# Re-ordering the five engines around the gene sums: projection a pair ahead, sums ahead of the turn of heads, and new orders behind the sums

## The reference

```
h = einsum('bg,egp->bep', x, weight * mask) + bias      # x 64x5000, weight 16x5000x128: 41 MB
h = h + attention(layernorm(h))   # 16 positions per batch row, 8 heads of 16 (+2 rotary), causal
h = h + ffn(layernorm(h))         # 64 experts, top 2 by gate, 128->64->128 silu, plus a shared expert
```

## Time and profile before

| | us |
|---|---|
| median of 3 runs (252.67 to 255.78) | 253.7 |
| the profiled execution's own time | 254.11 |
| its span (first to last instruction) | 252.4 |
| busy in the span: PE, DVE, POOL, ACT | 184.7, 152.0, 144.1, 82.4 |
| mean granted TensorE clock | 0.891 |

### The profile page before, as it was taken

The page is one execution under the profiler, slowest core; times in us unless marked ns, Lnnn a source line. Parts: engine busy times, 40 slices in busy tenths (PEclk is TensorE's granted clock), DMA queues, the critical chain, the costliest instruction groups (busy, mean ns, idle before and its releaser), DMA issues.

```text
span 252.4 us, 6075 instructions
## 1 busy us (share of the span) xinstructions
PE 184.7 (73%) x2479; PEld 153.9 (61%) x2479; DVE 152.0 (60%) x366; ACT 82.4 (33%) x245; POOL 144.1 (57%) x117
## 2 busy tenths in 40 slices
PE   0057877279989789695896699388976987999810
PEld 0057866169878678584785488257755766678410
DVE  0024382975696888979939928768796249011291
ACT  2004200023343333341331232538664444335500
POOL 3326479259979779999678783103114242074570
PEclk9999999977999999999599599657996599999965
DMA  7999999999999999999999999593011128213432
GB/s 237 256 342 418 361 421 334 403 417 417 417 419 422 417 419 416 426 417 413 396 226 220 227 194 145 153 265 145 4 42 52 55 70 243 87 42 96 139 96 53
DMA packets 32981, 65.11 MB, mean 258 GB/s; under 512 B 2874, under 2 KB 25367, under 8 KB 32375
## 3 DMA queue, kind: packets, MB, share of 16 engines
q1 hardware_dynamic: 31416, 59.47, 71.5%
q10 hardware_dynamic: 576, 3.26, 3.1%
q0 software_dynamic: 960, 1.97, 3.0%
HBM read 56.96 MB, written 7.73 MB: 256 GB/s over the span
## 4 chain that ended last, share of the span: by engine, by line
PE 39%; DVE 19%; DMA 16%; SPq 8%; ACT 7%; issue 4%; POOL 3%; POOLq 1%; DVEq 0%; ACTq 0%
DMA ring<-in_L_tok_weight_dram 15%; PE bank L833 13%; PE bank L1021 4%; SPq L360 4%; PE bank L991 4%; DVE bank L1233 3%; DVE prod L1227 3%; DVE ring L1206 3%; DVE prod L1251 2%; DVE bank L1259 2%; PE bank L1005 2%; SPq L366 2%; PE bank L971 2%; PE bank L876 2%; POOL ring L529 2%
## 5 line engine op out<-in xcount | busy, mean ns | idle before, releaser
L464 POOL TENSOR_TENSOR ring<-ring,mask 128x896 f32<-128x896 f32 (+1 forms) x48 | 91.6, 1933 | 19.0 <-DMA ring<-in_L_tok_weight_dram 19.0
L833 PE MATMUL bank<-ring,xT 128*64 128x128 f32 x1248 | 83.8, 294 | 9.9 <-DVE ring L1206 7.6
L833 PEld LDWEIGHTS bank<-ring,xT 128*64 128x64 f32 x1248 | 76.4, 149 | 14.6 <-DVE ring L1206 9.2
L1206 DVE TENSOR_TENSOR ring<-ring,bank 128x1024 f32<-128x1024 f32 (+1 forms) x45 | 45.7, 1049 | 35.5 <-DMA ring<-in_L_tok_weight_dram 35.5
L453 POOL TENSOR_TENSOR rstd<-mv,half 128x1 f32<-128x1 f32 (+1 forms) x24 | 14.2, 599 | 38.9 <-DVE mv L1214 23.4
L529 POOL DMA_INDIRECT ring<-expert_outputs,slot_index x16 | 16.0, 1002 | 16.9 <-DMA expert_outputs<-ring 8.0
L484 POOL DMA_INDIRECT expert_inputs<-xf,slot_index x14 | 14.3, 1021 | 9.9 <-DVE slot_index L1311 6.9
L814 PE MATMUL bank<-cst,w 64*128 64x64 f32 x39 | 5.3, 328 | 16.1 <-DMA w<-in_x_dram 15.4
L1021 PE MATMUL bank<-w2p,ring 64*64 64x128 f32 (+1 forms) x256 | 14.5, 291 | 3.4 <-ACT ring L705 2.1
L506 POOL TENSOR_TENSOR mask<-ring,mask 128x256 f32<-128x256 f32 x8 | 6.0, 756 | 16.3 <-ACT ring L699 16.3
L991 PE MATMUL bank<-w,ring 128*64 128x128 f32 (+1 forms) x256 | 14.9, 298 | 0.3 <-POOL mask L506 0.3
(11 more groups left out here) (151 smaller groups left out, 302.6 us busy)
## 6 DMA issues: line engine op xcount, KB each, us to landing
ring<-in_L_tok_weight_dram SPq DMA_DIRECT2D x48, 832.0 KB, 13.2
expert_inputs<-w ACTq DMA_DIRECT2D x3, 1024.0 KB, 9.9
ring<-expert_inputs SPq DMA_DIRECT2D x6, 512.0 KB, 5.4
expert_outputs<-ring SPq DMA_DIRECT2D x12, 256.0 KB, 2.3
mask<-in_L_tok_mask_dram SPq DMA_DIRECT2D x3, 832.0 KB, 16.1
w<-in_x_dram SPq DMA_DIRECT2D x1, 1250.0 KB, 13.6
w2p<-in_L_ffn_w_dram SPq DMA_DIRECT2D x1, 1024.0 KB, 18.9
xT<-masks_dram SPq DMA_DIRECT2D x1, 1024.0 KB, 7.9
```

What stands on the lines that cost most here:

```text
L464: pool.tensor_tensor(unit(j, q, SPLIT(q // 2), UC), unit(j, q, SPLIT(q // 2), UC), mask[:, (m + SPLIT(q // 2)) * D:(m + UC) * D], ALU.mult ...
L833: last = pe.matmul(bank[0][64 * par:64 * par + 64, 0:D], xT[:, (UC * t + c) * B:(UC * t + c + 1) * B], unit(j, 2 * t + par, c, c + 1), sta ...
L1206: dve.tensor_tensor(both(j, t, a, b), both(j, t, a, b), m.rearrange("p (u f) -> p u f", u=1).to_broadcast([P, 2, (b - a) * D]), ALU.mult). ...
```

## The change

Four things change, and no arithmetic does.

1. In the loop PE transposes and projects pair c-1 at the end of every turn (behind step 10, and behind step 11), where it did pair c-2 at the start. `turn_qk(b)` then stands at the start, `qkv(b)` behind the first step of sums and `values(b)` behind the second. ACT, DVE and POOL follow in their own orders. DVE's `scores` is split into `multiply_keys` and `sum_scores`, with `choose(d)` and `place(d)` between them.
2. From c = 5 on (`HEADED`) PE does step 0 of the sums ahead of `turn_o(d)`; for smaller c it stands behind `attend(d)`.
3. The orders behind the sums are new on PE, ACT, DVE and POOL. The experts' work stands further forward on PE.
4. The gathers of all five pairs of the first round are issued ahead of the wait for the last group (`GATHERED_EARLY` 4 to 5).

```
-GATHERED_EARLY = 4
+GATHERED_EARLY = NCH1          # 5
+HEADED = 5
-POOL_SHARE = (3, 3)
-VECTOR_SHARE = (2, 1, 2, 1)
+POOL_SHARE = (1, 1, 4)
+VECTOR_SHARE = (2, 2, 1, 1)
 ...                            # POOL, loop
                 mask_pieces(POOL_SHARE[0])
-                if d >= 0:
-                    root_h2(d)
                 if b >= 0:
                     root_qk(b)
                 mask_pieces(POOL_SHARE[1])
+                if d >= 0:
+                    root_h2(d)
+                mask_pieces(POOL_SHARE[2])
                 if c >= 1:
                     root_h(c - 1)
 ...                            # PE, loop
+                project_a, qkv_b, attend_d = c >= 1, b >= 0, d >= 0
+                if c >= HEADED:
+                    sum_genes(c, 0)
                 if attend_d:
                     turn_o(d)
-                if project_b:
-                    turn_xn(b)
+                if qkv_b:
+                    turn_qk(b)
                 if attend_d:
                     attend(d)
-                if project_b:
-                    project(b)
-                for n in range(4):
-                    sum_genes(c, n)
+                if c < HEADED:
+                    sum_genes(c, 0)
+                if qkv_b:
+                    qkv(b)
+                sum_genes(c, 1)
                 if attend_d:
                     turn_xf(d)
-                if project_b:
-                    turn_qk(b)
-                sum_genes(c, 4)
+                if qkv_b:
+                    values(b)
+                sum_genes(c, 2)
                 if attend_d:
                     gate(d)
-                if project_b:
-                    qkv(b)
+                sum_genes(c, 3)
                 if attend_d:
                     rank_tokens(d)
-                sum_genes(c, 5)
-                if project_b:
-                    values(b)
-                for n in range(6, 12):
+                for n in range(4, 12):
                     sum_genes(c, n)
-                    if c == NCH - 1 and n == 10:
+                    if project_a and n == 10:
                         turn_xn(c - 1)
-                if c == NCH - 1:
+                if c == 1:
+                    pe.wait_ge(s_centred, 2)
+                if project_a:
                     project(c - 1)
 ...                            # DVE, loop
-                mask_pieces(VECTOR_SHARE[2])
+                if a >= 0:
+                    stats_h(a)
+                if b >= 0:
+                    multiply_keys(b)
                 if d >= 0:
                     choose(d)
-                if a >= 0:
-                    stats_h(a)
+                mask_pieces(VECTOR_SHARE[2])
                 if d >= 0:
                     place(d)
                 if b >= 0:
-                    scores(b)
+                    sum_scores(b)
                     less_max(b)
```

More of the change, by code:

```diff
@@ L1236, in scores @@
                 then(dve.memset(raw(j)[0:64].rearrange("p (h s) -> p h s", h=NH)[:, :, n - 1:n], NEG))
+            def scores(j):
+                multiply_keys(j)
+                sum_scores(j)
             def less_max(j):
@@ L1391, in _ @@
             j, k, l = NCH - 3, NCH - 2, NCH - 1
+            weigh_values(j)
             stats_h(l)
-            heads(j)
-            scores(k)
+            sum_heads(j)
+            weights(0, NCH1)
+            multiply_keys(k)
+            sum_scores(k)
             less_max(k)
             add_attended(j)
-            heads(k)
-            scores(l)
+            weigh_values(k)
+            sum_heads(k)
+            multiply_keys(l)
+            sum_scores(l)
             less_max(l)
@@ L1401, in _ @@
             add_attended(k)
-            heads(l)
+            weigh_values(l)
+            sum_heads(l)
             place(j)
@@ L1420, in _ @@
             dve.tensor_scalar(flag_i[:], flag[:, 0:1], float(SLOTS), None, ALU.is_gt).then_inc(s_flag, 1)
-            for g in range(GROUPS1, GROUPS):
-                mid(g)
+            mid(8)
+            mid(9)
+            mid(10)
+            mid(11)
             shared_mid(0)
```

246 lines of the change are left out of this document (127 added, 119 removed).

## The result

The changed kernel is slower: 261.6 us (260.87 to 264.35, four runs) against 253.2 for the kernel before (four runs), a ratio of 1.038, interval 1.027 to 1.050. On a second chip it was 260.4 us and 1.027 (1.019 to 1.034). The forecast was 249 with a range to 257, so it missed on the other side. The profiled execution took 261.2 (span 259.5) where before took 254.11 (252.4): 7.1 more, where 4.5 less was forecast, a miss of 11.6 us.

What follows compares the result with a forecast made beforehand. Bound first by the granted clock, half speed in six stretches, then by TensorE. Loop +2.8, behind the sums 1.7 - 9.0 = -7.3, the end 0: -4.5 from 254.11 profiled gives 249.6, as median 249.2, said 249; range 242.3 to 257.

Steps and rivals of the forecast that it cites:

- E: End of the projection of pair k, closing the loop: 157.95 us before, forecast at 160.75.
- the rival: In the loop: TensorE falls to half clock behind waits at turn starts; three such turns cost 7.9 us, 257; chance 0.14.
- a case that was given 0.09: Whole kernel slower than before, above 258.8: the rival plus some of little gain from the orders behind the sums; chance 0.09.
- The loop's chain: Turns c = 3 to 7, put together from measured stretches: 16.2, 16.5, 16.8, 17.2 and 19.05 us, sum 85.75.
- The third turn (c = 2): In the loop: 4.3 us lost, as 2.9 idle, 0.7 transposing and projecting pair 1, 0.7 products at half clock.
- GpSimd's lateness in c = 7: In the loop: one mask ahead of root_qk(5) makes it start 1.55 us later, so c = 7 takes 19.05.
- its 2.8 us: End of the loop later than before: 4.3 - 1.45 = 2.8 us.
- The rows at no cost: Behind the loop: first round's rows requested at about 162, turn_xs(0) reached at 167.3; cost 0, at most 1 us.
- probs(k): On ScalarE behind the sums: standing behind silu(0) and silu(1), with more table loads, it costs 3.1 us.
- The stretch without the late rows: From E to turn_o(l): 35.4 us where it took 33.7, 1.7 later.
- From turn_o(l) to round two: Up to round two's first transposition: 15.4 us where it took 24.4, 9.0 less.
- Round two and the end: From round two's first transposition to the span's end: the 36.3 us stay, and part 4 gains nothing.

Runs made afterwards that it cites:

- e16: The changed kernel without part 2, step 0 behind attend(d) in every turn (HEADED = 8): 260.3 to 263.6 us, ratio to before 1.033.
- e4: The changed kernel with step 0 of the sums ahead of turn_o from c = 2 on: 260.0 us, ratio to before 1.015.
- e18: The changed kernel with two of the loads of w2 issued behind the loads of the first round's rows: 258.1 us, ratio to before 1.020.
- e9: The changed kernel with idle products sized to TensorE's waits at the start of turns 2 to 7: 257.1 us, ratio to before 1.013.
- e14: e9 with w2 also loaded in long rows, so the output is not the reference's: 256.7 us, ratio to before 1.012.
- e15: e10 with idle products in the old loop, ahead of turn_o in turns 5 to 7 and ahead of turn_qk(k): 248.5 us, ratio to before 0.981.
- e6: The changed kernel with TensorE's two short waits at the start of a turn filled with sums from c = 2 on: 259.9 us, ratio to before 1.028.
- e1: The kernel before with the new orders behind the sums and part 4, its old loop kept: 250.8 us, ratio to before 0.982.
- e10: e1 with mid(6) ahead of scatter(k) on GpSimd, nothing else: 249.3 us, ratio to before 0.981.
- e2: The changed kernel's new loop with the old orders behind the sums (parts 1 and 2 alone): ratio to before 1.011.
- e17: e15 with two loads of w2 issued behind the loads of the first round's rows, as in e18: 243.5 us, ratio to before 0.957.

## Why the prediction was wrong, step by step

**Where the miss of 11.6 us lies.** 6.4 us are in the loop (5.8 in turns 3 to 7, 0.6 ahead of them), 3.1 from E to turn_o(l), 1.4 from there to round two, 0.7 behind. The two steps that failed are the full clock assumed for `turn_qk`, `attend` and the steps of sums in each turn, and the cost of nothing put on the first round's rows.

**The half clock was the rival, and it was the case.** I gave it 0.14 because 2.33 us had left the clock full and 2.40 had not, and took my waits of 2.0 to 2.2 to be on the safe side. As a threshold on one wait this fails: it fell behind 2.05, and behind 0.84 and 0.66 together, and stayed behind 2.09 (e16), 1.33 with 0.66 (e4) and even 3.43 (e18). The rival's place and its decision rule were wrong, its size nearly right: 5.8 us over turns 3 to 7 (91.55 against 85.75), where it had 7.9. It stood at 257 in the forecast; 261.6 needed the late rows besides, a case that was given 0.09. The Trainium skill's rule, "TensorE: Matmul & The Clock Gate", section "HAM oscillation — how this bites in real kernels", that a loop which waits in each pass starts each pass cold, describes turns 2 to 4 here, though the example there has longer waits, for DMAs. The trace agrees in turns 2 to 4 (1.97 us for 1.09, behind 2.88, 2.61 and 2.05); in turns 5 to 7 the fall comes 1 to 2.4 us behind the second wait, in the middle of the chain.

**The loop's chain** was right once the clock was full: e9's five turns sum to 86.5, forecast 85.75. The third turn (c = 2), priced at 4.3, ended at 75.6, where 70.7 + 4.3 = 75.0 was meant, and c = 1 had already ended 0.9 later. This agreement holds only with the half clock in that turn, which the price had in part: in e14's execution without it the turn took 3.0 us less. GpSimd's lateness in c = 7 stood as said: `root_qk` starts right behind a mask, 19.0 us in e9 for 19.05. So at nearly full clock the new loop ends at 162.3 (e9), and the old one, with its waits filled too, at 155.0 (e15): the order of part 1 is the longer one by itself, as the forecast had said of it with its 2.8 us.

**The rows at no cost.** This step failed. I let the request for the last units come 7 us later and the transfers end at 163 to 165. But the weights are queued behind the request that the end of turn c = 5 releases, and that turn ended 12.9 us later (129.82 for 116.94): the late turns win time, the early ones have lost theirs by then. Of this the forecast had 7, by its own turns; the rest is for the most part the half clock again, which made turns 3 to 5 longer by 5.1 us. The transfers ended some 12 us later, and the request for the rows followed about 2 us behind (158 to 159.4 before, 170 to 171.9 after, 166 to 168.3 in e9; the ends are read from the DMA share in steps of 2 us). The step didn't hold even by its own numbers: with transfers that end at 163 to 165, a request 2 us behind them and the 4.3 us from request to `turn_xs(0)` (171.88 to 176.15), the rows are there at 169 to 171, and `turn_xs(0)` was to be reached at 167.3. That is a wait of 2 to 4 us, and 2.81 came; the forecast had shifted the request with E and not with the transfers. e18 shows the price: 38.5 to 35.3 us for the stretch.

**probs(k)** behind the silus cost 3.1 us in the forecast and 2.86 in the trace. The stretch without the late rows took 35.3 us in e18, 36.2 in e6 and 36.4 in e1, against 35.4: right to 1 us, and the 0.1 of e18 is luck.

**From turn_o(l) to round two** 15.4 was forecast, 16.8 came. `mid(6)` was put at 8.6 us behind turn_o(l) and ended at 8.4; the rest is the clock again (0.90 in the stretch), which falls behind the wait of 3.44: `up(7)` takes 1.46 us for 1.09. In e1 it falls there too, 1.3 us later. In e18, with the same orders and a wait of 3.43, it stayed at 1.00 and the stretch took 15.25. In e10, which took the wait away, it was 13.5.

**Round two and the end**, part 4 among them, changed by 0.7. The last gather starts 28.9 us behind the first transposition of round two, and 28.6 before: the gathers issued earlier gain nothing, as said. Part 4 was not run by itself.

**What stays open.** Why the clock falls behind waits of 0.8 and 0.7 in one turn and not behind 2.1 or 3.4 elsewhere; and the rest of what e1 and e2 together don't explain, beyond the 2 to 3 us of the rows. The new loop with both remedies, e9's idle products and e18's order of loads, was not run, so that the two causes make up the whole miss is argued from the stretches and not shown in one time.

## What to carry to other kernels

Price a wait of TensorE twice, once for itself and once for the products that follow at half clock, and don't take a short wait as safe because a slightly longer one was: compare TensorE's idle and busy time over a whole loop, before and after, at its granted clock. Where waits can't be removed, idle products sized to them (never longer) can be worth more than a new order: here they brought the end of either loop forward by about 4 to 5 us (e9, e15 against e1), though it reached the time only where the transfers behind the loop were in time too (e17). And when a loop's early turns get longer, look at which transfers their ends release, for a gain of the late turns doesn't bring these forward. A time that depends on such a transfer is to be shifted with the transfer, not with the end of the loop.

## What the hardware showed that I had not expected

- The granted clock fell to half behind two waits of 0.84 and 0.66 us in one turn (c = 5 of the changed kernel), and in e6 behind four waits of 0.23, 0.85, 0.30 and 1.60. It stayed full behind one of 3.43 in e18.
- Rows scattered by GpSimd while weights are in transfer land late: in the changed kernel the ten scatters in the loop took 3.9 to 8.5 us from issue to landing (median 5.9), the four behind it 2.2 to 2.7. With the weights' last loads put off (e18) the two that the first round waits for took 2.3 in place of 8.4 and 8.5.
- Issuing the second load of w13, whose pieces are 256 bytes, holds SyncE's queue for 12.5 to 15.5 us in every kernel; w2 in long rows was issued in 11.1 us for 16.5 and ended no earlier.
